# Building the fused image and word residual on chip, with the first norm in three groups of row tiles

## What is computed

```python
h = _L0_tok_ref(x, L0_tok_W, L0_tok_b)             # patches @ W.T + b: 8 images x 64 rows x 192
h = jnp.concatenate([h, _L0_txt_ref(x_txt, emb)], axis=1)   # + 77 word rows: 8 x 141 x 192
h = h + _L0_attn_ref(_layernorm(h), ...)           # begins with a second layernorm; two Mamba passes
h = h + _L0_ffn_ref(_layernorm(h), ...)
h = h + _L1_attn_ref(_layernorm(h), ...)
h = h + _L1_ffn_ref(_layernorm(h), ...)            # 8 experts, top 2
```

## Time and profile before

| | us |
|---|---|
| median of 3 runs | 780.86 |
| lowest, highest | 779.29, 783.02 |
| the profiled execution | 782.75 |
| its span in the trace | 780.9 |
| busy: PE, DVE, ACT, POOL | 647.4, 488.0, 367.5, 276.9 |

### The profile page before, as it was taken

One profiled execution on the slowest core, in us unless ns is written; L12 is line 12 of the kernel. 1 busy time (PEld: TensorE's weight loads), 2 busy tenths in 40 slices (PEclk: granted clock), 3 DMA queues, 4 the chain that ended last, 5 costly groups with the idle time before them and its releaser, 6 DMA issues.

```text
span 780.9 us, 13384 instructions
## 1 busy us (share of the span) xinstructions
PE 647.4 (83%) x4906; PEld 579.6 (74%) x4906; DVE 488.0 (62%) x1262; ACT 367.5 (47%) x846; POOL 276.9 (35%) x293
## 2 busy tenths in 40 slices
PE   2239898898899726448899999799989999999994
PEld 2229776578898612227788888698989999999994
DVE  2277779662331787681787785468538777877851
ACT  0027876861343436434656644342126655655541
POOL 3633515433020325002333232301131766756633
PEclk9758999995999956657999999879979999999998
DMA  7810000223000190200000002102064676787843
GB/s 219 184 43 4 2 1 1 92 85 98 1 1 1 53 225 0 91 21 4 2 4 7 4 5 83 45 1 112 10 244 136 177 245 200 218 248 201 213 128 67
DMA packets 30412, 67.89 MB, mean 87 GB/s; under 512 B 6890, under 2 KB 20755, under 8 KB 28011
## 3 DMA queue, kind: packets, MB, share of 16 engines
q0 software_dynamic: 13200, 48.20, 21.2%
q1 hardware_dynamic: 17147, 18.84, 8.8%
HBM read 60.90 MB, written 6.61 MB: 86 GB/s over the span
## 4 chain that ended last, share of the span: by engine, by line
PE 60%; DVE 12%; ACT 4%; issue 3%; POOL 2%; another core or an unknown queue 1%; POOLq 0%; DVEq 0%; ACTq 0%
PE bank L1812 10%; PE bank L1772 4%; PE bank L1776 4%; PE bank L1775 4%; PE bank L1774 4%; PE bank L1773 3%; PE bank L1695 2%; PE bank L1631 2%; PE bank L1674 2%; PE bank L1344 1%; PE bank L1485 1%; PE bank L1509 1%; PE bank L1510 1%; PE bank L1511 1%; PE bank L1403 1%
## 5 line engine op out<-in xcount | busy, mean ns | idle before, releaser
L2403 DVE TENSOR_SCALAR big<-bank 128x256 f32<-128x256 f32 (+1 forms) x126 | 52.1, 414 | 60.1 <-PE bank L1776 54.6
L1240 ACT ACTIVATE big<-bank 128x256 f32<-128x256 f32 (+1 forms) x126 | 47.7, 379 | 57.1 <-PE bank L1776 53.5
L796 POOL TENSOR_TENSOR big<-big,arc 128x423 f32<-128x423 f32 (+1 forms) x48 | 37.8, 816 | 77.4 <-DVE arc L2348 77.4
L823 POOL DMA_INDIRECT total<-big,goal x32 | 53.5, 1673 | 23.8 <-issue 17.3
L1772 PE MATMUL bank<-x_lead,w_lead 128*128 128x256 f32 x192 | 56.5, 294 | 0.1
L1775 PE MATMUL bank<-x_both,w_lead 128*128 128x256 f32 x192 | 54.5, 284 | 0.0
L1776 PE MATMUL bank<-x_both,w_rest 128*128 128x256 f32 x192 | 54.1, 282 | 0.0
L1774 PE MATMUL bank<-x_lead,w_rest 128*128 128x256 f32 x192 | 54.0, 281 | 0.0
L1773 PE MATMUL bank<-x_rest,w_lead 128*128 128x256 f32 x192 | 53.9, 281 | 0.0
L830 POOL DMA_INDIRECT big<-x_rows,origin x32 | 32.9, 1029 | 49.5 <-DVE goal L2460 23.1
L2414 DVE SCALAR_TENSOR_TENSOR big<-big 128x256 f32<-128x256 f32 (+1 forms) x126 | 50.2, 409 | 0.1
(11 more groups left out here) (530 smaller groups left out, 2014.8 us busy)
## 6 DMA issues: line engine op xcount, KB each, us to landing
big<-in_patches SPq DMA_DIRECT2D x1, 1536.0 KB, 7.6
areg<-in_e_gate_up SPq DMA_DIRECT2D x1, 1536.0 KB, 6.4
shared_lead<-in_e_gate_up POOLq DMA_DIRECT2D x1, 1536.0 KB, 6.9
wreg<-in_ffn_w SPq DMA_DIRECT2D x1, 1152.0 KB
ffw_lead<-in_ffn_w POOLq DMA_DIRECT2D x1, 1152.0 KB, 6.0
out<-total SPq DMA_DIRECT2D x2, 423.0 KB
wreg<-in_in_w SPq DMA_DIRECT2D x2, 419.0 KB
wreg<-in_in_w SPq DMA_DIRECT2D x4, 209.5 KB
```

The source lines that it names most:

```text
L823: pool.indirect_dma_start(out=total, in_=YS[:, j % 2, q * D:(q + 1) * D], in_offset=None, out_offset=bass.IndirectOffsetOnAxis(ap=goal[:, ...
L1240: nc.scalar.activation(GS[:, n % 3, 0:w], bank[2 * (n % 2)][:, 0:w], ACT.Silu).then_inc(S["g_silu"], 1)
L2403: v.tensor_scalar(UM[:, n % 3, 0:w], bank[2 * (n % 2) + 1][:, 0:w], 10.0, -10.0, ALU.min, ALU.max).then_inc(S["u_clip"], 1)
```

## The change

Image rows are moved into `H`'s row tiles by 11 float32 matmuls on PE (`place`), whose stationary operand is a window of a shifted identity; `shift_even` and `shift_odd` hold only the rows of the first or second batch of a pair. The results stay in PSUM. The token numbers and the flag for a match (`pick`, two columns) go through 13 more such matmuls, so that `ids` and `known` stand by row tile. POOL then gathers nine times 128 rows straight into place (`words`), and DVE writes `H = words * known + images` (`together`). The DRAM tensor `h0`, its eleven DMAs and SP's waits are gone.

The statistics, roots and normed rows are made for three groups of three tiles (`together`, `first_inverse`, `twice_normal`). The three groups have banks of their own. ACT writes the full precision tokens too (`first_tokens`, four operations for a group instead of two), and DVE only subtracts (`first_rests`). The first projection stands before the third group's transposes.

The loads of `shf` and patches are issued by ACT; `nxt` follows `tok_w` on SP; POOL issues the `in_lead` loads ahead of the gathers. POOL also makes the shifted identities (a memset and three selects of 128 x 384).

```diff
+        words = area(big3, TT * D, [P, TT, D])
...
-        XS1 = area(areg, TP, [P, 2, CM])
+        XS1 = [area(areg, TP, [P, 2, CM]), area(areg, 2 * TP, [P, 2, CM])]
...
+        IMG_AT = ((5, 0), (5, D), (7, 0), (7, D), (4, P), (4, P + D), (3, 0), (3, D), (2, 0))
+        IMG_BANK = (0, 1, 6, 0)
+        IMG_OUT, IMG_PLACED = (1, 2, 4, 6), (3, 5, 7, 8)
...
-            load(shf, window(76, 0, NX), "ld_tok")
-            load(nxt, window(NX, 1, 76), "ld_tok")
-            load(patches, i["patches"].rearrange("(k p) n -> p k n", p=P), "ld_embed")
             load(tokw, i["tok_w"].rearrange("(k p) n -> p k n", p=P), "ld_embed")
+            load(nxt, window(NX, 1, 76), "ld_next")
...
-            sp.wait_ge(S["img_ready"], 2)
-            for b in range(NB):
-                sp.dma_start(h0[b, 0:NI, :], img[(b % 2) * NI:(b % 2 + 1) * NI, b // 2, :]).then_inc(S["h_loaded"], 16)
-            sp.wait_ge(S["txt_ready"], 3)
-            sp.dma_start(h0[:, NI:L, :].rearrange("b n d -> n b d"), txt).then_inc(S["h_loaded"], 16)
-            sp.wait_ge(S["h_loaded"], 16 * (NB + 1))
...
-            sp.dma_start(H[:, 0:TT - 1, :], hf[0:(TT - 1) * P, :].rearrange("(t p) d -> p t d", p=P)).then_inc(S["h_loaded"], 16)
-            sp.dma_start(H[0:LAST, TT - 1, :], hf[(TT - 1) * P:T, :]).then_inc(S["h_loaded"], 16)
...
+            st.add(pool.memset(shift, 0.0))
...
-            pool.wait_ge(S["txt_ready"], 2)
-            for b in range(NB):
-                pool.indirect_dma_start(out=txt[:, b, :], out_offset=None, in_=i["emb"],
-                                        in_offset=bass.IndirectOffsetOnAxis(ap=ids[:, b:b + 1], axis=0))\
-                    .then_inc(S["gathered"], 16)
...
+            pool.wait_ge(S["txt_ready"], 3)
+            for t in range(TT):
+                pool.indirect_dma_start(out=words[:, t, :], out_offset=None, in_=i["emb"],
+                                        in_offset=bass.IndirectOffsetOnAxis(ap=ids[:, t:t + 1], axis=0))\
+                    .then_inc(gathered[t // 3], 16)
...
+            def second_deviations(g):
+                act.wait_ge(ln0_vx, g + 1)
+                nc.scalar.activation(std[:, TT + 3 * g:TT + 3 * (g + 1)], prod[:, 3 * g:3 * (g + 1)], ACT.Sqrt, bias=cst[:, 0:1]).then_inc(ln_std, 1)
+
+            def first_tokens(g):
+                act.wait_ge(ln_turned, g + 1)
+                if g == 2:
+                    act.wait_ge(S["xa_rest"], 2)
+                a, b = [bank[n] for n in ln_bank(0, g)]
+                wa, wb = ln1[:, 0, :], ln1[0:DB, 1, :]
+                cols = slice(g * CM, (g + 1) * CM)
+                nc.scalar.activation(XS1[g % 2][:, 0, :], a[:, 0:CM], ACT.Identity, scale=wa[:, 0:1], bias=wa[:, 1:2])
+                nc.scalar.activation(XAH[:, cols], a[:, 0:CM], ACT.Identity, scale=wa[:, 0:1], bias=wa[:, 1:2]).then_inc(ln_out, 1)
+                nc.scalar.activation(XS1[g % 2][0:DB, 1, :], b[0:DB, 0:CM], ACT.Identity, scale=wb[:, 0:1], bias=wb[:, 1:2])
+                nc.scalar.activation(XAB[0:DB, cols], b[0:DB, 0:CM], ACT.Identity, scale=wb[:, 0:1], bias=wb[:, 1:2]).then_inc(ln_out, 1)
+
+            nc.scalar.dma_start(shf, bass.AP(tensor=tok_in.tensor, offset=0, ap=[[1, 76], [76 + NX, NB], [1, NX]])).then_inc(S["ld_tok"], 16)
+            nc.scalar.dma_start(patches, patches_in.rearrange("(k p) n -> p k n", p=P)).then_inc(S["ld_embed"], 16)
             act.wait_ge(S["const_ready"], 9)
+            nc.scalar.activation(rss[:, 0:1], cst[:, 0:1], ACT.Sqrt)
+            deviations(0, ln_var, 3, ln_std)
+            second_deviations(0)
+            deviations(1, ln_var, 6, ln_std)
+            second_deviations(1)
+            deviations(2, ln_var, 9, ln_std)
             act.wait_ge(S["ld_inw"], 16 * 8)
-            ln(0, ln1)
+            first_tokens(0)
+            second_deviations(2)
+            first_tokens(1)
+            first_tokens(2)
...
+            pe.wait_ge(S["txt_ready"], 2)
+            parts = [(t, b, a - b * L - NI) for b in range(NB) for t, a, z in TXT_ROWS[b]]
+            for n, (t, b, row) in enumerate(parts):
+                at = P - (b * L + NI - t * P)
+                last = mm(bank[4][:, 2 * t:2 * t + 2], shift[0:NX, at:at + P], pick[:, b, :],
+                          start=n == 0 or parts[n - 1][0] != t, stop=n + 1 == len(parts) or parts[n + 1][0] != t)
+            last.then_inc(S["scoreT"], 1)
+
+            def place(j):
+                pe.wait_ge(S["img_ready"], j + 1)
+                for b in (2 * j, 2 * j + 1):
+                    for t, a, z in IMG_ROWS[b]:
+                        s_, at = (shift_odd, P + NI) if b % 2 else (shift_even, P)
+                        at -= b * L - t * P
+                        owners = [c for c in range(NB) for u, _a, _z in IMG_ROWS[c] if u == t]
+                        k, o = IMG_AT[t]
+                        last = mm(bank[k][:, o:o + D], s_[:, at:at + P], img[:, j, :], start=b == owners[0], stop=b == owners[-1])
+                last.then_inc(S["img_mm"], 1)
+
             pe.wait_ge(S["ld_embed"], 48)
             for j in range(NB // 2):
                 for k in range(KI):
-                    last = mm(bank[j // 2][:, (j % 2) * D:(j % 2 + 1) * D], patches[:, k, j * P:(j + 1) * P], tokw[:, k, :],
+                    last = mm(bank[IMG_BANK[j]][:, 0:D], patches[:, k, j * P:(j + 1) * P], tokw[:, k, :],
                               start=k == 0, stop=k == KI - 1)
-                if j % 2:
-                    last.then_inc(S["img_out"], 1)
-            pe.wait_ge(S["img_ready"], 2)
-            pe.wait_ge(S["txt_ready"], 2)
-            turn(0, XS)
-
-            pe.wait_ge(S["in_lead"], 16 * 6)
-            pe.wait_ge(S["in_rest"], 4)
+                last.then_inc(S["img_mm"], 1)
+                if j == 1:
+                    pe.wait_ge(S["txt_ready"], 3)
+                if j:
+                    place(j - 1)
+            place(NB // 2 - 1)
+            turn(0, XS, (0, 1))
...
+                if k == 0:
+                    turn(0, XS, (2,))
...
+            v.tensor_scalar(pick[:, :, 1], best[:, :], 128.0, None, ALU.is_ge).then_inc(S["txt_ready"], 1)
+            dve.wait_ge(S["scoreT"], 3)
+            st.add(v.tensor_copy(known[:, :], bank[4][:, 1:2 * TT:2]))
+            v.tensor_copy(ids[:, :], bank[4][:, 0:2 * TT:2]).then_inc(S["txt_ready"], 1)
+
+            def image(j):
+                dve.wait_ge(S["img_mm"], IMG_OUT[j])
+                if j == 0:
+                    dve.wait_ge(S["ld_embed"], 48)
+                v.tensor_tensor(img[:, j, :], bank[IMG_BANK[j]][:, 0:D], tokb, ALU.add).then_inc(S["img_ready"], 1)
+
+            def together(g):
+                dve.wait_ge(gathered[g], 48)
+                dve.wait_ge(S["img_mm"], IMG_PLACED[g + 1])
+                if g == 2:
+                    dve.wait_ge(S["padded"], 1)
+                for t in range(3 * g, 3 * (g + 1)):
+                    k, at = IMG_AT[t]
+                    r = rows(t)
+                    st.add(v.scalar_tensor_tensor(out=H[0:r, t, :], in0=words[0:r, t, :], scalar=known[0:r, t:t + 1], in1=bank[k][0:r, at:at + D],
+                                                  op0=ALU.mult, op1=ALU.add))
+                st.wait()
+                for t in range(3 * g, 3 * (g + 1)):
+                    st.add(v.bn_stats(stats[:, t, :], H[:, t, :]))
+                st.wait()
+                for t in range(3 * g, 3 * (g + 1)):
+                    v.bn_aggr(mv[:, t, :], stats[:, t, :]).then_inc(ln_var, 1)
+
+            def first_inverse(g):
+                w = slice(3 * g, 3 * (g + 1))
+                dve.wait_ge(ln_var, 3 * (g + 1))
+                dve.wait_ge(ln_std, 2 * g + 1)
+                st.add(v.reciprocal(rstd[:, w], std[:, w]))
+                st.wait()
+                st.add(v.tensor_tensor(prod[:, w], mv[:, w, 1], rstd[:, w], ALU.mult))
+                st.wait()
+                v.tensor_tensor(prod[:, w], prod[:, w], rstd[:, w], ALU.mult).then_inc(ln0_vx, 1)
+
+            def twice_normal(g):
+                w = slice(3 * g, 3 * (g + 1))
+                dve.wait_ge(ln_std, 2 * g + 2)
+                st.add(v.reciprocal(rstd2[:, w], std[:, TT + 3 * g:TT + 3 * (g + 1)]))
+                st.wait()
+                st.add(v.tensor_tensor(rstd2[:, w], rstd2[:, w], rstd[:, w], ALU.mult))
+                st.wait()
+                for t in range(3 * g, 3 * (g + 1)):
+                    v.tensor_scalar(XS[:, t, :], H[:, t, :], mv[:, t, 0:1], rstd2[:, t:t + 1], ALU.subtract, ALU.mult).then_inc(ln_x, 1)
+
+            def first_rests(g):
+                cols = slice(g * CM, (g + 1) * CM)
+                dve.wait_ge(ln_out, 2 * g + 1)
+                v.tensor_tensor(XR0[:, cols], XS1[g % 2][:, 0, :], XAH[:, cols], ALU.subtract).then_inc(S["xa_rest"], 1)
+                dve.wait_ge(ln_out, 2 * g + 2)
+                v.tensor_tensor(XAB[DB:P, cols], XS1[g % 2][0:DB, 1, :], XAB[0:DB, cols], ALU.subtract).then_inc(S["xa_rest"], 1)
...
```

(47 more changed lines are left out.)

83 lines of the change are left out of this document (27 added, 56 removed).

## The result

The changed kernel takes 791.93 us, the median of 4 runs (790.25 to 793.32), beside 780.3 us (779.29 to 783.02) for the kernel before on the same chip: a ratio of 1.0128 with a 95% interval of 1.010 to 1.0156. It is 1.3% slower; 769.6 was forecast, in a range of 764.5 to 776.5. The profiled execution has a span of 791.2 us, 10.3 more than the 780.9 of before.

The account below looks back on a forecast made before the run. H's trip through DRAM (13.4 us, PE idle) was taken as the bound. Summing the stage's steps put project(2) at 47.5 instead of 58.8, 11.3 us less, so 769.6 us, range 764.5 to 776.5.

Parts of the forecast that it names:

- everything behind `project(2)` moves with it: From project(2) PE streams without a gap, so its shift, 11.3 us earlier, carries to the end one for one.
- The matmuls that move the picks: On PE after picking: 26 records at 0.21 us each, 5.5 us, until 19.6.
- The gathers: On POOL from 20.3: nine of 128 rows at 1.31 us each, groups landing at 26.0, 30.0 and 33.9.
- rival C: Gathers' many fetches of row 0 queue up, nothing left from 2.8 us per gather, a loss beyond; chance 0.04.
- a DRAM trip that was real: Before the statistics: writing H to DRAM, waiting and reading back cost 13.4 us with PE idle.
- Tokens: Token loads at the start: two instead of three needed at 76 GB/s, there at 7.2 instead of 8.53.
- Picking: From tokens to end of picks on DVE: 6.75 us, unchanged but for one 0.15 us flag instruction, done at 14.1.
- in_lead: Loads now ahead of POOL's gathers: 1.7 MB, 5.9 us, issued some 13 us before the first gather, not felt.
- Rival B: Loads collide while gathers run, 2.2 us per gather, together(2) at 41.8 instead of 36.0: 775.4 us; chance 0.06.
- Images: PE's patch and place matmuls from 19.6: records 0.31 us at first, then 0.155, place(1) done at 28.3.
- rival A: PE later through delayed handovers or a clock staying at 1.2 GHz, together(0) 2.3 to 5.4 us later: 771.9 to 775.0; chance 0.20.
- ... and are covered: POOL's subtractions for the weights' rests, 1.95 us each, run from 32.1 to 39.9 beside the norm at no cost.

Follow-up runs that it names:

- between_dve: Changed kernel with nxt loaded ahead of tok_w, in_lead loads held until the picks are done, weight subtractions on DVE between image additions: 770.1 us, ratio 0.9952.
- nxt_early: Changed kernel with one edit, SP issues the load of nxt ahead of tok_w: 778.6 us, ratio 0.9968.
- before_inlead: Kernel before with one edit, its six in_lead loads issued ahead of its eight gathers: 784.0 us, ratio 1.0125.
- nxt_again: Repeat on another chip of the changed kernel with nxt loaded ahead of tok_w: 773.8 us, ratio 0.9999.
- one_input: Changed kernel with the norm's small products made by tensor_scalar, one tensor input instead of two from SBUF: 790.9 us, ratio 1.0105.
- lead_between: Changed kernel with nxt loaded ahead of tok_w and in_lead loads issued only when picks are done, still ahead of the gathers: 774.0 us, ratio 0.9988.
- inlead_late: Changed kernel with one edit, the six in_lead loads issued behind the gathers again: 787.6 us, ratio 1.0061.
- all_three: Changed kernel with nxt ahead of tok_w, in_lead loads behind the gathers, and small products with one tensor input: 783.9 us, ratio 1.0009.

## Why the prediction was wrong

*Right.* That everything behind `project(2)` moves with it: the table has the two columns within 0.6 us for all losses and within 2.1 us for the gains, over a spread of 15 us. The gains arrive a little smaller, by 0.1 to 2.1 us. The matmuls that move the picks: 5.71 us for 26 records, 5.5 forecast. The gathers: 1.26 us each instead of 1.31, and the packets of the nine end between 37.3 and 47.3, so nothing queues for row 0, and rival C is out (it needed 2.8). The gain left in `between_dve` (4.6 us at `project(2)`) fits a DRAM trip that was real, as I had said; no run puts that trip back alone.

*Tokens, 2.8 us.* I timed `cur` and `shf` by the 76 GB/s of the earlier trace rows and left out the wide loads now issued beside them: `tok_w` at 1.22 and `patches` at 1.40, which before stood behind all three token loads. 10.04 instead of 7.2. `nxt_early`, with all three token loads ahead of `tok_w`, has them at 8.79, so two loads for three had saved nothing. No run holds the patches back alone.

*Picking, 11.3 us: the step that failed.* I wrote that from tokens to picks was "unchanged but for one flag instruction". It was not (18.2 us instead of 6.9): the picks wait for `nxt`, which the diff puts behind `tok_w` and on a semaphore of its own. The line stands in the diff, and I never asked when that load would land. Taken alone, the edit `nxt_early` gives 12.9 us back at `project(2)`.

*"in_lead", within the same wait.* I checked the earlier `in_lead` loads only against the first gather, 13 us after them, and not against loads already in flight. In `before_inlead` this one edit costs 10.2 us, with the longer multiplication (4.0 us) in it; in after it makes up 7.1 of the 11.4 us, as long as `nxt` is in its late place. Rival B had the right mechanism (loads collide) and the wrong place: it priced the gathers, which stayed at 1.26, and not the loads ahead of the picks.

*Images, 3.4 us.* About a third of this is rival A's clock part. The rate of 0.155 us per record came later than the 11 records I counted: in after the windows count 15 records from 33.8 to 37.8 and 10 from 37.8 to 39.8. The 24 records took 6.69 us, against 3.7 + 1.9 = 5.6 by my sum. In `nxt_again` they take 6.96 us, and there the whole stretch is 10.3; so about 1.5 of the 3.4 us belong to every run of this order, and 1.9 to after and `one_input`, open as said. Rival A's own price was miscounted: up to `place(1)` there are 44 records (three pairs of 12, twice 4), not 32, so a slow clock throughout would have cost 32 x 0.155 = 5.0 us and not 3.1.

*"... and are covered", 4.3 us: the second step that failed.* I let POOL's subtractions run beside the norm at no cost, because no result of theirs was awaited. They do have a cost: the product L1978 (L1979 in `lead_between`) ends within 0.1 us of POOL's last subtraction in after, `nxt_early`, `nxt_again` and `lead_between`, wherever it begins, and it is 0.16 us where POOL does not subtract. The kernel before ran them from 35.13 to 42.8, in DVE's idle stretch, a condition that I never wrote down. The Trainium skill (SBUF — State Buffer, Who interferes with whom) states this rule: a DVE instruction with two SBUF inputs contends with a GpSimd instruction that reads SBUF, and one of them fully blocks; `tensor_scalar` can enter a mode that contends too. The traces agree on both forms (L1978 4.42, L1991 4.57). They differ in how long: in four kernels the block of L1978 lasts past the end of the instruction that was running, until the last of POOL's back-to-back subtractions, over three of them in after and `lead_between`. In `inlead_late` it lasts until the running one ends (L1978 1.71, L1980 1.87), and in `all_three` the three normed tiles get in one by one. What decides between the two stays open. A small `tensor_scalar` of one column was not held at all (0.64 us for three).

The chance for slower was 0.03, all of it on rival C. It was far too small, because each addition had been priced by itself against engines; what the loads do to each other was priced only for the gathers.

## What to carry to other kernels

When a diff reorders loads, list for each load what is issued ahead of it and beside it until it lands, and who waits for it; a small load that gates a chain belongs ahead of every wide one, and a wide one that nobody needs yet belongs behind. "Covered" is a claim about time and about neighbours: check which instructions will run beside which, before and after the shift, above all GpSimd's beside DVE's with two inputs from SBUF. Before work is moved to an idle engine, look up when its inputs land.
